# Cross attentions with a one-pass output projection, queries partly in memory and the context addition on ScalarE; the experts' first lists and last block

## What is computed

```
q_hk    = layernorm(x) @ Wq.T                      # 32 batches of 32 tokens, 16 heads of 128
q_big   = einsum('bshk,hkq->bshq', q_hk, w_kc_q)
kv      = rope(ctx_512)                            # 257 positions of 128 for each batch
scores  = einsum('bhsr,bhlr->bhsl', q_big @ W_qr, kv @ W_kr)
ctx_c   = softmax(scores) @ kv                     # 16 heads of 128
x      += einsum('bhsd,hkd->bshk', ctx_c, w_kc_kv).reshape(...) @ Wo.T
```

```
for each expert: out += (silu(x @ Wg.T) * (x @ Wu.T)) @ Wd.T * share[:, expert]
```

## Time and profile before

| | |
|---|---|
| median of 3 runs | 2144.7 us (2143.73 to 2145.28) |
| the profiled execution | 2146.89 us, its span 2145.1 us |
| mean granted clock of TensorE | 0.981 |
| TensorE busy | 2035.0 us, 95% of the span |
| VectorE, ScalarE, GpSimd busy | 54%, 37%, 45% |
| attention of L0x, of L1x | about 119 to 405.7 us; 1120 to 1414.9 us |
| self attention L1a | 1414 to 1607 us |
| experts | 1607 to 2145 us |

### The profile page before, as it was taken

How to read it: one execution, slowest core, us unless ns; L and a number is a source line. 1 busy time by engine, 2 the same in 40 slices (tenths; PEclk the granted TensorE clock), 3 DMA queues, 4 the chain that set the end, 5 groups by cost and what they waited for, 6 DMA issues and landing times. The chain is left out here.

```text
span 2145.1 us, 27878 instructions
## 1 busy us (share of the span) xinstructions
PE 2035.0 (95%) x8746; PEld 1371.8 (64%) x8746; DVE 1163.7 (54%) x2698; ACT 798.7 (37%) x1986; POOL 955.7 (45%) x929
## 2 busy tenths in 40 slices
PE   7999999998999999999998999999978999999995
PEld 6867676686588744666656676667654555555552
DVE  4258888366561122555547788759863434444442
ACT  2354443143411200333335434335524444445441
POOL 1265573211252100577768656366303444555552
PEclk9999999999999999999999999999987999999998
DMA  5220011300211100111122000110344999888886
GB/s 195 99 80 23 23 28 39 80 2 1 100 58 53 34 1 0 32 50 41 55 88 63 25 21 25 63 67 1 104 150 138 307 301 327 211 215 210 215 208 167
DMA packets 83391, 209.19 MB, mean 98 GB/s; under 512 B 13728, under 2 KB 39840, under 8 KB 74752
## 3 DMA queue, kind: packets, MB, share of 16 engines
q1 hardware_dynamic: 60528, 153.54, 20.8%
q0 software_dynamic: 21280, 51.38, 11.7%
q10 hardware_dynamic: 1440, 2.49, 0.3%
HBM read 257.95 MB, written 34.36 MB: 136 GB/s over the span
## 5 line engine op out<-in xcount | busy, mean ns | idle before, releaser
L98 PE MATMUL banks<-L1f_w,L1f_xT 128*128 x760 | 265.3, 492 | 2.6 <-issue 1.3
L2673 POOL DMA_INDIRECT moe_sums<-L1f_y,L1f_row x95 | 150.6, 1585 | 221.6 <-DVE L1f_is_who L2542 150.6
L159 POOL TENSOR_TENSOR rstd<-rstd,power 128x1 f32<-128x1 f32 x48 | 28.6, 596 | 399.3 <-DVE rstd L153 399.3
L98 PEld LDWEIGHTS banks<-L1f_w,L1f_xT 128*128 128x128 f32 x760 | 138.0, 192 | 83.1 <-issue 7.8
L2681 POOL DMA_INDIRECT L1f_xg<-moe_rows,L1f_row x95 | 94.2, 991 | 64.8 <-DVE L1f_row L2537 37.7
L2509 DVE SCALAR_TENSOR_TENSOR L1f_z<-banks,L1f_share,L1f_sg 128x192 f32<-128x192 f32 x95 | 39.7, 418 | 148.5 <-ACT L1f_sg L2444 148.4
L461 PE MATMUL banks<-L0x_wn,L0x_qT 128*128 128x512 f32 x256 | 115.1, 593 | 0.8 <-DVE x L531 0.8
L461 PE MATMUL banks<-L1x_wn,L1x_qT 128*128 128x512 f32 x256 | 115.1, 593 | 0.8 <-DVE x L531 0.8
L98 PE MATMUL banks<-L0f_down,L0f_z 128*128 128x512 f32 x256 | 111.1, 592 | 1.5 <-DVE L0f_z L2000 1.5
L2444 ACT ACTIVATE L1f_sg<-banks 128x192 f32<-128x192 f32 x95 | 31.4, 330 | 206.9 <-PE banks L98 206.9
L98 PE MATMUL banks<-L0f_hT_hi,L0f_ug_hi 128*128 128x512 f32 x256 | 100.0, 391 | 0.0
(11 more groups left out here) (402 smaller groups left out, 5258.5 us busy)
## 6 DMA issues: line engine op xcount, KB each, us to landing
L1f_w<-in_experts SPq DMA_DIRECT2D x95, 1280.0 KB
L1f_laid<-moe_counts SPq DMA_DIRECT2D x59, 512.0 KB, 5.4
w<-in_L1x_heads SPq DMA_DIRECT2D x16, 704.0 KB, 4.0
w<-in_L0x_heads SPq DMA_DIRECT2D x8, 1216.0 KB, 5.2
w<-in_wug SPq DMA_DIRECT2D x8, 1024.0 KB, 4.8
L0x_craw<-in_ctx SPq DMA_DIRECT2D x96, 64.0 KB, 2.1
L1x_craw<-in_ctx SPq DMA_DIRECT2D x96, 64.0 KB, 2.0
w<-in_L0x_out SPq DMA_DIRECT2D x4, 1280.0 KB, 5.6
```

The costliest lines, as they stand in the source:

```text
L98: ins = pe.e.matmul(out, w, m, start=first and n == 0, stop=last and n == len(pairs) - 1)
L159: pool.e.tensor_tensor(self.rstd[:, i:i + 1], self.rstd[:, i:i + 1], self.power[:, 0:1], ALU.pow).then_inc(self.rstd_set.sem, 1)
L2673: pool.e.indirect_dma_start(self.sums[j % 2][:, :], bass.IndirectOffsetOnAxis(ap=self.row[:, j:j + 1], axis=0), self.y[j % self.NY][:], No ...
```

## The change

1. **Output projection.** The folded matrices and the contexts are kept as halves. ScalarE copies the upper half of a part (`split_hi`, 128x512), VectorE makes the lower (`split_lo`), into memory that lies over the queries; a part is then 12 one-pass products instead of 4 full ones. VectorE also makes the lower halves of the 16 folded matrices (`folded_lo`). The folds up front use four banks in turn, and each waits for both halves of the one that had its bank.
2. **Queries in memory.** `qT` holds four tiles. Queries of tiles 4 to 7 go to small buffers (`away`) and by DMA to DRAM (`send`); after tile i's projection they come back into its place (`take_back`, four DMAs of 1 MB, 512 bytes at a time).
3. **Context addition.** VectorE's L518 becomes an activation (identity, with bias) on ScalarE, behind its other work of the step.
4. **The self attention's start** is spread over the last steps: ScalarE makes one weight's upper half behind each of the last copies, VectorE one operation at a time. Its memory is laid out anew; for L1a only one of the five buffers is cleared early, four behind the first `pow` of the heads' norms (L1736).
5. **Experts, first lists:** the first five blocks' counts alternate between two pairs of banks.
6. **Experts, last block:** block 94 isn't added through memory; its halves are multiplied with a matrix of ones and zeros (`find_goal`, 128x1024) onto the 8 tiles. The even sums are read once block 92 is added, the odd sums in four pieces once block 93 is.

```diff
@@ LatentAttention @@
+    def fold_bank_of(self, h):
+        return self.sh.psum((3, 6, 4, 5)[h % 4])
+    def folds_kept(self, eng, n):
+        eng.wait_ge(self.wn_hi, n)
+        eng.wait_ge(self.wn_lo, n)
...
+            if n < 2:
+                self.send(sp, away + n)
...
+            if b >= 12 and b % BPT == 0 and b // BPT - 3 < self.HALF:
+                self.take_back(sp, b // BPT - 3)
             if self.FIRST + b == NSLOT * OUT_HEADS:
                 self.out_w[NSLOT].load(sp)
             if b + 2 < B:
                 self.load_context(sp, b + 2)
...
+    def take_back(self, sp, i):
+        self.sent_all(sp)
+        sp.wait_ge(self.projected, BPT * (i + 1))
+        sp.wait_ge(self.q_back, 16 * i)
+        sp.e.dma_start(self.qT[:, i, :, :], self.far[:, :, i * P:(i + 1) * P]).then_inc(self.q_back.sem, 16)
...
     def project_out(self, pe, i, part):
+        o = BPT * i + part
         if part == 0:
             pe.wait_ge(self.x_set, i)
-        pe.wait_ge(self.wn_set, XH)
-        pe.wait_ge(self.ctx_set, (i + 1) * BPT)
-        for h in range(4 * part, 4 * part + 4):
-            ins = pe.e.matmul(self.o_bank, self.qT[:, i, h, :], self.wn[:, h, :], start=h == 0, stop=h == XH - 1)
-        if part == BPT - 1:
-            ins.then_inc(self.projected.sem, 1)
+        self.folds_kept(pe, XH)
+        pe.wait_ge(self.part_hi_set, o + 1)
+        pe.wait_ge(self.part_lo_set, o + 1)
+        both = (self.part_hi[o % 2][:], self.part_of(self.ctx_lo, o))
+        accumulate(pe, self.o_bank, [p for n in range(4) for p in parts(
+            cut(both, slice(None), slice(n * P, (n + 1) * P)), cut(self.wn, slice(None), 4 * part + n))],
+            first=part == 0, last=part == BPT - 1).then_inc(self.projected.sem, 1)
@@ scalar_attention, at the end of a step @@
-        self.after.halves_hi(act)
+            if 0 <= b - self.LAG_VALUES < B:
+                self.keep_context(act, b - self.LAG_VALUES)
+            o = b - self.LAG_VALUES - BPT + 1
+            if 0 <= o < BPT * NT:
+                self.split_hi(act, o)
+            if o > self.LAST and o < self.LAST + BPT:
+                self.after.halves_hi(act, o - self.LAST - 1)
+
+    def split_hi(self, act, o):
+        act.wait_ge(self.ctx_set, BPT * (o // BPT + 1))
+        act.wait_ge(self.projected, o - 1)
+        act.e.copy(self.part_hi[o % 2][:], self.part_of(self.qT, o)).then_inc(self.part_hi_set.sem, 1)
+
+    def keep_context(self, act, b):
+        act.wait_ge(self.mixed, b + 1)
+        act.e.activation(self.of_batch(b), self.c_bank, ACT.Identity,
+                         bias=self.kvT[b % self.NKT][:, LC * P:LC * P + 1]).then_inc(self.ctx_set.sem, 1)
@@ vector_attention @@
         for b in range(B + self.LAG_VALUES + BPT):
+            o, t = b - self.LAG_VALUES - BPT, b - self.LAG_TURN
+            if o >= 0:
+                self.split_lo(dve, o)
             if b < B:
                 self.find_peak(dve, b)
             if 0 <= b - 1 < B:
                 self.weigh(dve, b - 1)
-            if 0 <= v < B:
-                dve.wait_ge(self.mixed, v + 1)
-                dve.e.tensor_scalar(self.of_batch(v), self.c_bank, self.kvT[v % self.NKT][:, LC * P:LC * P + 1], None,
-                                    ALU.add).then_inc(self.ctx_set.sem, 1)
...
+            if self.FIRST + b < XH:
+                self.folded_lo(dve, self.FIRST + b, self.o_bank)
+            if self.LAST <= o < self.LAST + BPT - 1:
+                self.after.halves_lo(dve, o - self.LAST)
...
+    def split_lo(self, dve, o):
+        dve.wait_ge(self.part_hi_set, o + 1)
+        dve.e.tensor_tensor(self.part_of(self.ctx_lo, o), self.part_of(self.qT, o), self.part_hi[o % 2][:],
+                            ALU.subtract).then_inc(self.part_lo_set.sem, 1)
@@ SelfAttention.gpsimd @@
-        pool.e.memset(self.vbd[2][:], 0.0).then_inc(self.cleared.sem, 1)
...
+            if i == 0:
+                for tile in self.clear_late:
+                    pool.e.memset(tile[:], 0.0).then_inc(self.cleared.sem, 1)
@@ Experts @@
+    def limit_banks(self, j):
+        return self.sh.psum(6 if j < self.AHEAD and j % 2 else 0, 2)
...
-        pe.wait_ge(self.seen, j)
+        pe.wait_ge(self.seen, j - 1 if j < self.AHEAD else j)
...
+        sp.wait_ge(self.added[0], 16 * self.adds(0))
         for i in range(NT):
             sp.e.dma_start(self.sh.x[:, i, :], self.sums[0][i * P:(i + 1) * P, :]).then_inc(self.even_back[i].sem, 16)
+        sp.wait_ge(self.added[1], 16 * self.adds(1))
+        for n, signal in enumerate(self.odd_back):
+            sp.e.dma_start(self.h[:, 2 * n:2 * n + 2, :], self.sums[1][2 * n * P:(2 * n + 2) * P, :].rearrange(
+                "(i p) n -> p i n", p=P)).then_inc(signal.sem, 16)
...
+    def spread_last(self, pe):
+        pe.wait_ge(self.goes_to, 1)
+        pe.wait_ge(self.last_hi, 1)
+        pe.wait_ge(self.last_lo, 1)
+        pe.wait_ge(self.y_set, self.LAST)
+        for i in range(NT):
+            places = self.upto[:, i * P:(i + 1) * P]
+            accumulate(pe, self.sh.psum(i), [(places, part) for part in self.last_parts()]).then_inc(self.by_row.sem, 1)
```

More of the change, by code:

```diff
@@ L244, in __init__ @@
         self.after = None
-        self.qT = self.sb("qT", [P, NT, XH, P])
+        with ExitStack() as part:
+            self.qT = self.sb("qT", [P, self.HALF, XH, P], F32, part)
+        self.ctx_lo = self.sb("ctx_lo", [P, self.HALF, XH, P], F32R)
+        self.far = sh.nc.dram_tensor(f"{name}_far", (P, XH, self.HALF * P), F32, kind="Internal").ap()
     def sb(self, n, shape, dt=F32, arena=None):
@@ L265, in attention_memory @@
         self.small = [sb(f"small4_{i}", [P, 5, 4]) for i in range(4)]
+        self.wn = tuple(sb(f"wn_{v}", [P, XH, D], F32R) for v in ("hi", "lo"))
+        self.part_hi = [sb(f"part_hi{i}", [P, BANK], F32R) for i in range(2)]
         self.s_bank = [sh.psum(i) for i in range(3)]
@@ L293 @@
     LAG_TURN, LAG_VALUES = 2, 3
+    HALF = NT // 2
     NKT = 5
@@ L316, in sync_attention @@
         for b in range(B):
+            if b == (0 if first_context else 2):
+                for n in range(away + 2, self.UNITS):
+                    self.send(sp, n)
+            if b >= 12 and b % BPT == 0 and b // BPT - 3 < self.HALF:
+                self.take_back(sp, b // BPT - 3)
             if self.FIRST + b == NSLOT * OUT_HEADS:
@@ L585, in __init__ @@
         self.queries = [(self.q0_set, 2 * n), (self.q1_set, 2 * n)]
+        self.sent = [take(f"expert_landed{i}", 16 * len(range(i, n, 2))) for i in range(2)]
         self.head_w = [sh.add_weights(sh.d[f"{name}_heads"][g], self.width, [
@@ L882, in __init__ @@
         self.queries = [(self.q_set, n)]
+        self.sent = [take(f"expert_landed{i}", 16 * len(range(i, XH, 2))) for i in range(2)]
         self.head_w = [sh.add_weights(sh.d[f"{name}_heads"][h], self.width,
@@ L1155, in row_buffers @@
             return [tuple(sb(f"hT_{v}{i}", [P, KD, P], F32R) for v in ("hi", "lo")) for i in n]
-        def tables():
-            self.mask = sb("mask", [P, S])
-            if normed:
-                self.cosg, self.sing = sb("cosg", [P, 2, DH]), sb("sing", [P, 2, DH])
-                self.gam = sb("gam", [P, 4, DH])
-            else:
-                self.bias = {key: sb(key, [P, n]) for key, n in (("bq", D), ("bk", kw), ("bv", vw), ("bo", D))}
-            self.kbd = [sb(f"kbd{i}", [P, groups, BPT, P]) for i in range(2)]
-            self.vbd = [sb(f"vbd{i}", [P, BPT, groups, P]) for i in range(3)]
@@ L1178, in __init__, with pair, halves @@
-        self.qkv = [[sb(f"{key}{i}", [P, n]) for i in range(3)] for key, n in (("qn", D), ("kn", kw), ("vn", vw))]
+        def pair(key, shape):
+            return [sb(f"{key}{w}", [P, *shape]) for w in range(2)]
+        def halves(key, n):
+            return tuple(sb(f"{key}_{v}", [P, KD, n], F32R) for v in ("hi", "lo"))
+        self.hT, self.w_q = row_buffers(range(2)), halves("wq", D)
+        if normed:
+            self.sq, self.part_c = pair("sq", (D,)), pair("part_c", (AH, DH))
+            q_rows = []
+        else:
+            self.hT += row_buffers(range(2, 3))
+            q_rows = pair("qn", (D,))
@@ new lines, in __init__ @@
+        self.w_k, self.w_v = halves("wk", kw), halves("wv", vw)
+        if normed:
+            self.part_s = pair("part_s", (AH, DH))
+            self.hT += row_buffers(range(2, 3))
+        self.mask = sb("mask", [P, S])
+        if normed:
+            self.cosg, self.sing = sb("cosg", [P, 2, DH]), sb("sing", [P, 2, DH])
+            self.gam = sb("gam", [P, 4, DH])
+        else:
+            self.bias = {key: sb(key, [P, n]) for key, n in (("bq", D), ("bk", kw), ("bv", vw), ("bo", D))}
+        self.clear_early = [sb("kbd0", [P, groups, BPT, P])]
@@ L1358, in sync @@
         self.w[3].load(sp)
+        self.begin(sp)
     def tensor(self, pe):
@@ L2474, in see @@
         act.wait_ge(self.planned, 1)
-        counts, n = self.limit_banks(), j - self.LAID
```

(1 more changed line is left out.)

194 lines of the change are left out of this document (132 added, 62 removed).

## The result

| | before | changed |
|---|---|---|
| median | 2144.99 us (4 runs, 2143.73 to 2147.92) | 2122.47 us (4 runs, 2119.97 to 2122.96) |
| ratio | | 0.9891, 95% interval 0.9874 to 0.9908 |
| span of the profiled execution | 2145.1 us | 2120.8 us |
| mean granted clock | 0.981 | 0.981 |

The account below looks back on a forecast made before the run. TensorE's list of work was taken to bound the attention's middle (8.27 us a step), chains its edges. Attentions -19.7, L1a +3, experts -4.5 and -6 gave -27 us: 2117.5 us from the median 2144.7, range 2102 to 2140.

Parts of the forecast that it names:

- Rival 4: Whole kernel: the middle gains as forecast, but edges cost double and experts' ends give half, 2134 us; chance 6%.
- The projection: Attention's steady steps: twelve one-pass products replace four full ones, step 8.27 to 7.77 us on average, -14 us per attention.
- the ring: Steady step: chain through ScalarE's exponents, context addition and copy, then VectorE's lower half and peaks; 7.34 us, 7.92 with collisions.
- Rival 1: Attention's middle: the ring or VectorE takes TensorE's place, so the middle gains nothing, +1 us, 2145.5; chance 8%.
- VectorE's sum: Steady step: VectorE's work, without the context addition and with the lower half, is 6.3 to 6.9 of 7.67 us, not binding.
- Rival 2: Steady steps: lower half suffers collisions and handovers cost more, or the addition needs table loads; some +18 us, 2163; chance 8%.
- rival 3: Attentions: reads of queries delay the context loads, 3 us for each of 8 reads, 24 us, 2141; chance 4%.
- The attention's end: Last parts of each attention: shorter products save 2.4 us, waits before two parts cost 1.8 and 2.0; together +1.4.
- The start: First steps of each attention: each fold of weights has two readers in sequence; +3 us in L0x, +2.5 in L1x.
- L1a: Self attention's first tiles: four memsets behind GpSimd's first root make the second tile's products late; +3 us, bounds 0 and 5.5.
- The experts' start: First five lists: with two pairs of banks the period falls from 2.52 to 1.30 us; -4.5 us, bounds -2 and -7.
- The experts' end: Last block: reads of the sums begin earlier, 4 MB take 13 us from 2119.3; -6 us, bounds -3 and -9.

Follow-up runs that it names:

- Experiment 1: The changed kernel without the two products with a lower half in each part of the output projection: 2107.98 us (one run), steps 7.48 and 7.62 us.
- experiment 2: The changed kernel with the context addition put back on VectorE, behind its scaling, all else the same: 2126.41 us (one run).
- experiment 5: The changed kernel with contexts asked for before queries, first five lists on one pair of banks, both sums read after block 93: 2126.58 us (one run).
- Experiment 3: The changed kernel with lower halves ahead of statistics in all tiles: 2123.19 us; only at the seventh tile, with GpSimd's subtraction held back: 2108.93 us.
- Experiment 4: The changed kernel with L1a's late memsets behind the second root: 2118.12 us; on VectorE: 2115.23; two behind each of two roots, with attention's-end edits: 2103.93.

## Why the prediction was right, and where it wasn't

**The sum** was -27 on the profiled span, the trace says -24.3. The sign, the place (the steady steps) and the size of each attention (-9.6 and -10.1 forecast, -9.4 and -9.6 measured) hold. But each attention is a sum whose terms missed in opposite directions: over both, the middle and the start came out 3.4 and 3.5 us better than forecast and the ends 7.6 worse. That these cancel is luck. Rival 4, dearer edges and cheaper gains at the experts' ends, came about in part and is hidden in the total by the middle's surplus.

**The projection.** "A step would be 7.67" was the list alone; it is 7.60, since the products follow the transpositions with hardly a gap. The allowance for collisions in the ring (7.77) was not needed: the ring stayed under TensorE's list. Term forecast -14, measured -15.9 and -15.5. The lower bound of the gain does not follow from its own words: twelve products at 0.24 and a gap of 0.2 at both ends leave 3.43 - 3.28 = 0.15 us, not 0.33, so the bound of the term would be -4 and not -9; the measured value lies far from either. Experiment 1 shows that its room is small, as forecast, but that it is not the ring alone. Rival 1 didn't come about, but the others' pace (7.5 to 7.6 by experiment 1) is close under TensorE's.

**VectorE's sum**, 6.3 to 6.9 of 7.67, came out as 6.8 to 7.0. The use that was made of it afterwards (experiment 2: 8.0, so VectorE binds) was wrong: the step stayed at 7.60.

**The context addition** costs ScalarE 1.24 and hides. Rival 2, in its part on table loads, is out. **The reads of queries** hide; rival 3 is out (experiment 5).

**The attention's end** is the term that was mis-sized most: +1.4 forecast with a bound of +4, measured +4.9 and +5.5. Both idle times were named with their causes, at about their lengths. Two costs were missing: the slow products behind an idle time, 1.7 us twice in L0x and 2.9 once in L1x, and in L1x VectorE's lower half held by GpSimd's subtraction (2.09 us for 0.69, idle time 3.41 for 2.01). These make up about the 3.5 and 4.1 us that the term missed. Experiment 3 shows both: with the orders mended the lower half takes 0.68 and no product is slow.

**The start** was forecast +3 and +2.5, measured +1.6 and +0.4, both within their bounds. One of its parts is shown: with the addition back on VectorE the start is 3.3 and 3.5 us longer (experiment 2), so that relief is real; which of the others was priced too high is open.

**L1a** was right in size by a wrong step. The prediction said that GpSimd's roots come late; what costs is VectorE's normalisation, held until the memsets end. Experiment 4 moved the hold, took it away (at the price of VectorE's own memsets), and shortened it. Against 104.1 us, the first brought 0.8 us, the second nothing and the last 3.6.

**The experts' start**: -4.5 forecast, -3.2 in the trace and 3.3 by experiment 5. Behind the fifth list TensorE's first rows had to land, which TensorE now waits for (1.5 us), so not all of 4 x 1.2 us counts.

**The experts' end**: -6 forecast, -3.2 measured. The step that was mis-sized is "4 MB at 320 GB/s take 13 us from 2119.3". They took 16.9, from 2098.4 to 2115.3. The rate was about right, but other traffic shared the engines: until 2105.2 block 93's sums, 0.26 MB, took 30% of the 16 DMA engines' time, and behind 2105.2 the stores of finished tiles 21%. Block 93's sums landed after 7.1 us and not 4.7, and the odd sums are read only then; VectorE's eight additions and the stores, 9.5 us, still stand behind their first piece. By the other traces of this code the gain is nearer 4 us than 3.2 (25.2 at the median, against 29.2 in the one trace of before).

The -1.8 us within the experts' blocks was not forecast, and no run tests it. In the traces of the variants the same stretch is 0.2 to 2.2 us shorter than before, so it may be scatter.

## What to carry to other kernels

A part of a list that is shortened in the steady state pays by its full length only while the next chain is shorter; here the two nearly met at 7.6 us. Price a stage's end by chains, and add to each idle time of TensorE of 2 us or more the slow products that may follow it (1.7 to 2.9 us in the changed kernel, three times of four). And before an operation on SBUF tensors is given to VectorE, look at what GpSimd runs at that moment: not the sum of both but the end of GpSimd's run of instructions can set when it is done.

## What the runs showed of the hardware that was not expected

VectorE is **held, not slowed**, by some instructions of GpSimd. A normalisation of 128x512 (0.55 us at the median, 0.95 in this place of the kernel before) took 5.31 or 5.32 us in all nine traces in which it met a row of four memsets of 1.80 us each: it began beside the second and ended 0.3 us behind the fourth, and was not let in between them. With two in a row it was 1.8, again until 0.3 us behind the last. A lower half of 128x512 (0.69) took 5.04 and 2.09 us beside GpSimd's subtraction of 5.6 us, as it began 1.1 or 4.1 us into it, and ended 0.5 us behind it both times. Which pair meets matters: beside the memsets, operations with two SBUF tensors kept their 0.68 to 0.69. By the Trainium skill ("VectorE: DVE Perf Modes", section "Two Vector instructions with no wait between them") the second SBUF read interface of VectorE is shared with GpSimd. The runs agree for the lower half, which reads two SBUF tensors, and for the peaks, which read PSUM and beside GpSimd's products took 1.28 us for two, no more than elsewhere. That a memset, which reads nothing, holds the normalisation longest is not told by that sentence, and no run here shows how it comes about.

TensorE's granted clock fell to the lower level behind many of its idle times at an attention's end, for some 3 to 7 us, and not behind others of the same length. Over the twelve traces of the changed kernel and its variants, counted before parts 28 and 31:

| idle time, us | times | the clock fell behind it |
|---|---|---|
| 1.3 to 1.6 | 11 | 0 |
| 2.0 | 6 | 2 |
| 2.6 | 14 | 11 |
| 3.4 to 5.5 | 9 | 9 |

So the longer the idle time, the more often slow products follow; for one of 2.0 or 2.6 us it can go either way from one execution to the next of the same code (before part 28 of L1x the changed kernel kept 1.00 in its first trace and fell in its second). That the slow products come from GpSimd's or the DMAs' work beside them is not borne out: in L1x they ran at 0.50 with both idle (1389 to 1392, shown above).
